# A gated recurrence on TensorE: the update gate's low-weight products made narrower and moved ahead of a wait

## What is computed

```
def step(H, xs):
    xz, xr, xh = xs
    Z = sigmoid(xz + H @ Whz.T + bhz)          # update gate
    R = sigmoid(xr + H @ Whr.T + bhr)          # reset gate
    H_tilda = tanh(xh + (R * H) @ Whh.T + bhh) # candidate
    H_new = Z * H + (1 - Z) * H_tilda
    Y = H_new @ Whq.T + bhq
```

## Time and profile before

| | |
|---|---|
| device time, median of 3 runs | 1223.15 us (1220.16 to 1224.41) |
| profiled execution, first to last instruction | 1218.6 us |
| TensorE matmuls, busy | 1211.4 us (99%), 22464 |
| TensorE weight loads, busy | 1169.6 us (96%) |
| VectorE, busy | 870.8 us (71%) |
| ScalarE, busy | 449.4 us (37%) |

### The profile page before, as it was taken

The page is one execution under the profiler, slowest core; times in us unless marked ns, Lnnn a source line. Parts: engine busy times, 40 slices in busy tenths (PEclk is TensorE's granted clock), DMA queues, the critical chain, the costliest instruction groups (busy, mean ns, idle before and its releaser), DMA issues.

```text
span 1218.6 us, 54017 instructions
## 1 busy us (share of the span) xinstructions
PE 1211.4 (99%) x22464; PEld 1169.6 (96%) x22464; DVE 870.8 (71%) x5774; ACT 449.4 (37%) x2256; POOL 59.8 (5%) x45
## 2 busy tenths in 40 slices
PE   9999999999999999999999999999999999999998
PEld 8799999999999999999999999999999999999975
DVE  5277777777777777777777777777777777777665
ACT  2233333333333333333333333333333333333332
POOL 2100000000000000000000000000000000000000
PEclk9999999999999999999999999999999999999999
DMA  9411100111110011110011101011111011001000
GB/s 349 188 25 30 29 16 16 29 30 29 30 26 7 28 29 30 29 30 8 24 29 30 29 30 22 10 29 29 30 29 30 4 28 29 29 29 25 3 7 11
DMA packets 43285, 43.97 MB, mean 36 GB/s; under 512 B 7432, under 2 KB 39696, under 8 KB 41760
## 3 DMA queue, kind: packets, MB, share of 16 engines
q1 hardware_dynamic: 40720, 39.70, 11.5%
q10 hardware_dynamic: 2256, 0.76, 0.2%
q0 software_dynamic: 64, 0.07, 0.0%
HBM read 35.83 MB, written 4.69 MB: 33 GB/s over the span
## 4 chain that ended last, share of the span: by engine, by line
PE 98%; DMA 1%; DVE 0%; SPq 0%; issue 0%; ACT 0%; DVEq 0%
PE bank L375 54%; PE gate_rh L375 31%; PE gate_z L375 13%; DMA l1w<-in_l1w 1%; ACT rg L800 0%; DVE rhp L1102 0%; DVE state L1118 0%; ACT hin L800 0%; SPq L271 0%; SPq L280 0%; SPq L282 0%; DVE low L1239 0%; SPq L281 0%; SPq L277 0%; SPq L278 0%
## 5 line engine op out<-in xcount | busy, mean ns | idle before, releaser
L800 ACT ACTIVATE rg<-gate_rh 128x16 f32<-128x16 f32 x512 | 93.8, 183 | 445.6 <-PE gate_rh L375 445.6
L375 PEld LDWEIGHTS gate_rh<-state,whp 128*128 128x128 f16 x6144 | 237.5, 96 | 14.4 <-DVE state L1118 8.1
L375 PE MATMUL gate_rh<-state,whp 128*128 128x8 f16 x6144 | 243.4, 167 | 1.0 <-DVE state L1118 0.6
L375 PEld LDWEIGHTS gate_rh<-rhp,whp 128*128 128x128 f16 x6144 | 228.0, 96 | 14.2 <-DVE rhp L1102 8.0
L375 PE MATMUL gate_rh<-rhp,whp 128*128 128x8 f16 x6144 | 234.9, 167 | 0.6 <-DVE rhp L1102 0.3
L1102 DVE SCALAR_TENSOR_TENSOR rhp<-rg,hist 128x16 f16<-128x16 f32 x512 | 90.0, 176 | 159.4 <-ACT rg L800 142.3
L375 PE MATMUL gate_z<-state,whp 128*128 128x16 f16 x4096 | 179.7, 176 | 0.0
L800 ACT ACTIVATE zg<-zsum 128x16 f32<-128x16 f32 x512 | 110.4, 216 | 166.9 <-DVE zsum L1107 166.9
L375 PE MATMUL bank<-xt,rw 128*128 128x128 f32 x1024 | 166.3, 292 | 0.0
L375 PE MATMUL bank<-ge,rw 128*128 128x128 f32 x1024 | 165.3, 290 | 0.0
L1118 DVE TENSOR_TENSOR_SCAN state<-zin,hin 128x32 f16<-128x32 f32 x512 | 114.9, 224 | 68.8 <-ACT hin L800 3.4
(11 more groups left out here) (159 smaller groups left out, 1616.0 us busy)
## 6 DMA issues: line engine op xcount, KB each, us to landing
gates<-gates_t SPq DMA_DIRECT2D x30, 512.0 KB, 5.4
aw<-in_aw SPq DMA_DIRECT2D x4, 2048.0 KB, 23.4
out<-osb SPq DMA_DIRECT2D x32, 128.0 KB, 3.0
xt<-in_xT SPq DMA_DIRECT2D x30, 128.0 KB, 5.4
rw<-in_rw SPq DMA_DIRECT2D x2, 1024.0 KB, 9.9
sw<-in_sw SPq DMA_DIRECT2D x3, 512.0 KB, 6.2
wh<-in_wh SPq DMA_DIRECT2D x3, 256.0 KB, 12.2
wx<-in_wx SPq DMA_DIRECT2D x3, 256.0 KB, 19.7
```

Source lines behind the costliest of these rows:

```text
L375: return pe.matmul(o, w, x, start=start, stop=stop, skip_group_check=True)
L800: return act.activation(o, i, f, **kw)
```

## The change

Two functions take the place of `update_gate` in every step but the first. The four matmuls with the weights' low half now read the state's high half alone (8 columns instead of 16, into the first of the two sums), and they stand ahead of the wait for the state's low half and ahead of the reset gate's last four matmuls. The four with the weights' high half are as before. The product of the two low halves is left out of the update gate. The number of matmuls is the same: 20 from the start of a step to `z_done`. `r_done` was signalled by the 12th of them and is now signalled by the 16th; `z_done` is still signalled by the 20th.

```
+            def update_low_weights(par, now):
+                for half in range(KC):
+                    for k in range(KC):
+                        mm(z_ps[par][:, 0, half, now], whp[:, 1, Z, k, half * P:(half + 1) * P], state[:, k, :, 1], False, False)
+
+            def update_high_weights(par, now):
+                for half in range(KC):
+                    for k in range(KC):
+                        i = mm(z_ps[par][:, :, half, now].rearrange("p a c -> p c a"), whp[:, 0, Z, k, half * P:(half + 1) * P],
+                               state[:, k], False, True)
+                return i
...
                 pe.wait_ge(st_hi, n)
                 recur(pr, R, 0, parts, 1)
                 recur(pr, R, 1, parts, 1)
+                update_low_weights(par, now)
                 pe.wait_ge(st_low, n)
                 recur(pr, R, 0, parts, 0, r_done)
-                update_gate(par, now).then_inc(z_done, 1)
+                update_high_weights(par, now).then_inc(z_done, 1)
```

## The result

The changed kernel takes 1260.22 us (median, 1256.53 to 1260.83, 4 runs) against 1223.78 us for the kernel before beside it (1220.16 to 1224.57, 4 runs): a ratio of 1.0307, 95% interval 1.0286 to 1.0327. The forecast was 1259.4 us, and 1254.8 us for the span of the profiled execution, which is 1254.8 us. Both profiled executions are, by their spans, the shortest of their kernel's four; the other three of the changed kernel have spans of 1258.0 to 1259.0 us.

The account below looks back on a forecast made before the run. TensorE's stream and the chain r_done, rg, rhp, rhp's low half, h_done were taken to bound together. 30.6 + 5.6 = 36.2 us on a 1218.6 us span gives 1254.8, plus 4.55 to the median: 1259.4 us, range 1252 to 1267.

Parts of the forecast that it names:

- The point it hung on: TensorE's stream and the chain from `r_done` through `rhp`'s low half arrive together; delaying `r_done` delays `h_done` in full.
- Narrowing at 0: Four update-gate matmuls cut from 16 to 8 columns keep the 0.025 us pitch, so cost 0.
- Change of the PSUM tile at 0: Three tile changes between reset and update runs instead of one: taken as 0, with 5 us kept for the range.
- 306 steps at 0.100 us, 30.6: Steps behind a filler of eight have no wait to fill; `r_done` comes four pitches, 0.100 us, later: 30.6 us.
- 185 steps at 0.030 us, 5.6: Steps behind a filler of six: the wait is filled, yet `r_done` comes 0.030 us later: 5.6 us.
- 20 steps at 0: Late-starting steps, where the filler has run out: the 13th matmul awaits the same event, so `r_done` does not move: 0 us.
- The last step of the sum: From the 1254.8 us span to the runs' median: 4.55 us added, giving 1259.4 us.
- The update gate's earlier sum is worth nothing: Sum ready 0.07 us sooner behind six gains nothing, since `zsum` stands on VectorE behind `rhp` and `rh`.
- The wait as the bound: Rival: TensorE's stream sets the pace, so filling the wait gains 16 us, giving 1207 us; chance 0.04.
- the half-hidden case: Rival: only `rhp`'s high half counts, so losses and gains nearly cancel, -3 us, giving 1220 us; chance 0.04.
- The second kind alone: Rival: room behind fillers of eight absorbs the 0.100 us; only 5.6 us remain, giving 1229 us; chance 0.03.
- The clock: Rival: TensorE's pauses of about 0.1 us in most steps lower its clock, giving 1282 us and up; chance 0.02.

Follow-up runs that it names:

- the chain cut: Candidate's last four products reread `rhp`'s high half, not waiting for its low half: kernel before 0.9956 (1217.96 us), changed kernel 0.9987 (1221.41 us).
- Behind the wait: Changed kernel with the four narrow products placed after the wait for the state's low half, ahead of the reset gate's last four: 1.0441, 1278.87 us.
- the two products placed ahead only behind six: Changed kernel with only two narrow products ahead of the wait, only in steps behind a second filler of six: 0.9998, 1223.35 us.
- the runs with one kind of step: Changed order only in steps behind a second filler of six (1.0050, 1228.93 us) or only behind one of eight (1.0245, 1254.70 us).
- the kernel without the update gate's four: Narrowed-not-moved kernel without the update gate's four products with the weights' low half: 0.9997, 1224.69 us.
- behind six alone: Changed kernel with the new order only behind a second filler of six; elsewhere narrow products stand behind `r_done`: 1.0050, 1228.93 us.
- reset gate four less: Kernel before without the reset gate's four products with the weights' low half, which stand ahead of `r_done`: 0.9737, 1191.69 us.

## Why the prediction was right

- *The point it hung on*, that TensorE's stream and the chain from `r_done` arrive together at the candidate's ninth matmul: shown from both sides. Time taken from TensorE behind `r_done` brings nothing (0.9997), time taken ahead of it brings 2.6%, and with the chain cut the change costs 3.4 us. That the two meet within 0.005 us comes from how long this kernel's first fillers happen to be: where that filler is shorter, the candidate's run waits.
- *Narrowing at 0*: shown (0.9993, 0.9982 to 1.0005). *Change of the PSUM tile at 0*: the groups of the changed kernel start at the bare pitch, so the 5 us kept for it weren't needed.
- *306 steps at 0.100 us, 30.6*: 30.3 in the traces, and 0.0245 timed with these alone. *185 steps at 0.030 us, 5.6*: 5.7 in the traces, and 0.0050 timed. *20 steps at 0*: 0.0. Behind the wait, where no step has anything to fill, it is 0.103 us in all three kinds.
- *The last step of the sum*, 4.55 us from the span to the median of the runs: 5.42 us were measured (1260.22 - 1254.8). Part of it is that the profiled execution of the kernel before was one of its short ones, and that the changed kernel's was too is luck, as is the agreement of the spans to 0.1 us: the terms were rounded to 0.005 us a step, some 2 us in all.
- *The candidate's busy sum* was to be some 270 us and is 278.1; the 0.54 us a run forecast beside it give 276.
- *The update gate's earlier sum is worth nothing*: shown by the two products placed ahead only behind six (0.9998).
- *Rivals.* The wait as the bound and the half-hidden case are out by the result and by the runs with one kind of step; what the half-hidden case assumed, that only `rhp`'s high half counts, was made true in the chain cut, and there the change does cost next to nothing. The second kind alone would have been 1229 us; the kind behind eight carried five sixths. The clock was 1.00 through the profiled recurrence of the changed kernel, with its pauses of 0.1 us a step. Its three other executions have a mean of 0.998, which would be some 5 us at half clock (an estimate: 0.002 x 2 x 1259), so the rival is out as a cause of 36 us, but not every execution was free of a fall.

No version came out that beats both kernels with the whole computation. The fastest, at 1191.69 us, leaves out a part of the reset gate's product.

## What to carry to other kernels

Filling a wait on the busiest engine is worth something only if the work that fills it doesn't stand ahead of a signal that another engine waits for: count how far the signal moves, not how short the gap gets. Even without that it brings nothing while a chain over other engines ends last (0.9998 above). Where short matmuls overlap in the profile, busy shares hide waits of nearly their drawn length; compare the lengths of equal runs instead, and look for a time between two events of a chain (here `rg` to `hin`) that is the same whatever the filler. To find which side of a balanced loop has slack, leave out the same small piece of work ahead of the signal in one run and behind it in another.

## What the hardware showed beside that

In six of the twelve profiled executions the granted clock fell to half once in the midst of the work, 75 to 78 us into the span. This is the kernel without the update gate's four (stretch, length, busy us of each engine, granted clock):

```profile
70.00:77.10 7.10, 6.52 (x123) 6.08 (x122) 5.19 (x36) 2.66 (x14) 0.00 (x0) 1.00 0.25 50
77.20:80.50 3.30, 3.30 (x41) 3.18 (x40) 1.30 (x10) 1.14 (x5) 0.00 (x0) 0.50 0.60 99
80.60:84.00 3.40, 3.40 (x57) 3.32 (x56) 1.96 (x13) 1.15 (x6) 0.00 (x0) 1.00 0.00 0
```

TensorE's matmuls covered 92% of the 7.10 us ahead of the fall to 1.2 GHz and all of the stretch in it, in which 41 were done against 57 in the next, about as long. With the products moved behind the wait the low stretch was longer:

```profile
75.30:92.30 17.00, 17.00 (x213) 16.46 (x212) 6.72 (x45) 4.56 (x23) 0.00 (x0) 0.50 0.16 34
```

The kernel before in the same stretch:

```profile
75.30:92.30 17.00, 17.00 (x332) 16.84 (x331) 11.40 (x75) 6.36 (x33) 1.67 (x1) 1.00 0.05 15
```

It did 332 matmuls where the other did 213. By the step lengths above, the 17 us at half clock cost about 5.5 us of the profiled span (an estimate: 58.2 - 52.6).

The start of the span differs too. In four executions (the kernel before, the changed one, behind six alone, reset gate four less) the trace has the clock at full from 4.2 to 4.6 us on, and the recurrence's first matmul stands at 55.3 to 55.6 us. In the other eight it is at full only from 10.1 to 13.1 us on, and the first matmul stands at 57.2 to 58.7 us. A matmul of 512 columns shows it: it takes 0.38 us at 5.61 us in the kernel before and 0.59 us at 5.84 us in the kernel without the update gate's four. All six executions with the later fall are among these eight, none among the four; whether the one has to do with the other isn't shown. What brings the fall about is open; no run was made for it.
